# A transformer block with self and cross attention: preparing stage and first pass as one stage, and a new order of the loop

## The reference

```python
h1 = _ln(x, n1_g, n1_b)
x = _attn(h1, h1, q1, k1, v1, o1_w, o1_b, heads) + x
h2 = _ln(x, n2_g, n2_b)
x = _attn(h2, context, q2, k2, v2, o2_w, o2_b, heads) + x
h3 = _ln(x, n3_g, n3_b)
proj = h3 @ ff_w1 + ff_b1
a, g = jnp.split(proj, 2, axis=-1)
ff = a * jax.nn.gelu(g, approximate=False) @ ff_w2 + ff_b2
return ff + x
```

## Time and profile before

| | us |
|---|---|
| median of 3 runs | 1505.35 (1504.9 to 1515.25) |
| profiled execution | 1509.97 |
| its span, first to last instruction | 1508.2 |

### The profile page before, as it was taken

How to read it: one execution, slowest core, us unless ns; L and a number is a source line. 1 busy time by engine, 2 the same in 40 slices (tenths; PEclk the granted TensorE clock), 3 DMA queues, 4 the chain that set the end, 5 groups by cost and what they waited for, 6 DMA issues and landing times. The chain is left out here.

```text
span 1508.2 us, 36412 instructions
## 1 busy us (share of the span) xinstructions
PE 1390.9 (92%) x13777; PEld 1261.9 (84%) x13777; DVE 888.5 (59%) x2175; ACT 649.8 (43%) x1454; POOL 381.3 (25%) x473
## 2 busy tenths in 40 slices
PE   4599489999999999999999999999856999999999
PEld 1599467888888888889888888888746999999999
DVE  5666137777777677777777776776525434242421
ACT  2234123455555555555555555555433322223231
POOL 8221111212212212212122122122006423333341
PEclk9799779999999999999999999999867999999999
DMA  3365534444444455454453443442112010101000
GB/s 103 103 229 204 185 113 125 116 131 138 113 128 138 121 145 148 130 153 134 139 151 112 125 141 107 133 133 85 55 33 72 10 40 10 35 13 31 13 9 23
DMA packets 127678, 155.62 MB, mean 103 GB/s; under 512 B 29016, under 2 KB 123424, under 8 KB 127520
## 3 DMA queue, kind: packets, MB, share of 16 engines
q1 hardware_dynamic: 127520, 153.47, 34.1%
HBM read 62.98 MB, written 28.93 MB: 61 GB/s over the span
## 5 line engine op out<-in xcount | busy, mean ns | idle before, releaser
L684 DVE TENSOR_REDUCE neg_max<-score 100x1 f32<-100x361 f32 (+1 forms) x800 | 409.0, 535 | 212.3 <-PE score L509 107.7
L882 ACT ACTIVATE probs<-expin 120x400 f32<-120x400 f32 (+2 forms) x640 | 302.5, 504 | 144.1 <-PE expin L534 138.0
L534 PE MATMUL expin<-qs,ks 128*120 128x200 f32 (+2 forms) x1280 | 261.1, 293 | 12.1 <-DMA qs<-max_parts 10.8
L534 PEld LDWEIGHTS expin<-qs,ks 128*120 128x120 f32 (+2 forms) x1280 | 191.0, 184 | 54.0 <-ACT probs L882 26.1
L509 PE MATMUL score<-ks,qs 128*100 128x362 f32 x640 | 207.5, 349 | 6.4 <-DMA qs<-q_parts 3.6
L1626 DVE SCALAR_TENSOR_TENSOR hidden<-ps_a,b_cols,gelu 128x320 f32<-128x320 f32 x100 | 55.1, 551 | 169.0 <-PE ps_a L1549 165.2
L951 POOL TENSOR_TENSOR var_eps<-mv,eps 100x1 f32<-100x1 f32 x32 | 6.1, 192 | 526.8 <-DVE mv L751 526.8
L1792 POOL TENSOR_TENSOR hid_lo<-hidden,hid_hi 128x320 fp32r<-128x320 f32 x100 | 88.0, 881 | 130.9 <-ACT hid_hi L1703 130.9
L509 PEld LDWEIGHTS score<-ks,qs 128*100 128x100 f32 x640 | 103.2, 170 | 14.7 <-issue 10.4
L1715 ACT ACTIVATE gelu<-ps_g,b_cols 128x320 f32<-128x320 f32 x100 | 52.8, 528 | 137.6 <-PE ps_g L1549 137.5
L555 PE MATMUL attn<-probs,vc 120*17 120x100 f32 (+1 forms) x3840 | 111.2, 256 | 0.1
(11 more groups left out here) (180 smaller groups left out, 3070.0 us busy)
## 6 DMA issues: line engine op xcount, KB each, us to landing
ks<-kc_parts SPq DMA_DIRECT2D x192, 181.0 KB, 2.5
qk_dram<-qk_parts SPq DMA_DIRECT2D x32, 500.0 KB, 4.1
qs<-q_parts SPq DMA_DIRECT2D x192, 75.0 KB
ks<-qk_dram SPq DMA_DIRECT2D x96, 125.0 KB
qs<-qk_dram SPq DMA_DIRECT2D x192, 62.5 KB
ks<-kc_parts SPq DMA_DIRECT2D x96, 90.5 KB, 2.2
ctx_raw<-in_ctxT SPq DMA_DIRECT2D x32, 180.5 KB, 2.8
ctx_raw<-in_ctxT SPq DMA_DIRECT2D x64, 90.2 KB, 2.9
```

What stands on the lines that cost most here:

```text
L534: mm = pe.matmul(dst, ks[a][u][:, c, j0:j0 + n], qs[a][u][:, :, q_slot(c) if a == 2 else c, :], start=True, stop=True)
L684: nc.vector.tensor_reduce(dst, src, AX_X, ALU.max, negate=True).then_inc(max_made, 1)
L882: nc.scalar.activation(probs[e % NPT][0:n, :], expin[e % 2][0:n, 0:HG * N], ACT.Exp, scale=SCALE)\
```

## The change

**One stage in place of two.** `first_stage` loads x and the q, k and v weights at once. The first layer norm's gain and bias are now applied to the tokens (`scale`: two SCALAR_TENSOR_TENSORs with `g_rows` and `b_rows`), so the weights are only split. The other weights are loaded and split between the groups (`context_low`, `second_bias_low`, `q2_gain`, `out_low`, `q2_low`), and GpSimd clears the stacks between its small steps. The split features live in the room of the cross key stacks. After groups 3 and 5 the own stacks of batches 0 and 1 are loaded (`load_own`, 9 DMAs, also used in the loop), and the stage no longer waits for its last stores.

**The loop.** The cross queries are made as rows (8 matmuls of 320 columns), copied by ScalarE into `q2_rows` and turned by three transposes (`QT`). Cross scores are made for two heads at a time and self scores for ten, in one pair of banks; a maximum is taken over the pair, and the next pair waits for it. There are 11 `probs` instead of 8, context takes 2 DMAs instead of 3, and all orders are new.

**The feed-forward's start** no longer waits for the x2 stores before it, gets gain and bias rows ahead of the other tiles, waits for each vector by itself, loads ScalarE's Gelu table early, and adds `ff_b2` on GpSimd later.

```diff
-NW, NPT = 3, 8
+NW, NPT = 3, 11
...
+def load_own(sp, b, qk1_dram, v1_dram, qs, ks, vs, zeros, landed):
+    clear_max(sp, qs, zeros, landed)
+    src = qk1_dram[b]
...
+    sp.dma_start(vs[:].rearrange("p h d -> p (h d)"), v1_dram[b]).then_inc(landed, 16)
+OWN = 9
...
-        w_q2 = sb("w_q2", [P, 6, DP], F32R)
+        w_q2 = sb("w_q2", [P, 6, D], F32R)
...
-        score = [ctx.enter_context(nc.psum_tensor(f"score{i}", [P, 512], F32)) for i in range(2)]
+        score = ctx.enter_context(nc.psum_tensor("score", [P, 2, 512], F32))
...
-                sp.dma_start(ctx_raw[0:64, 1, 0:J], c[P:C]).then_inc(ctx_landed, 16)
-                sp.dma_start(ctx_raw[64:P, 1, 0:J], c[P:C]).then_inc(ctx_landed, 16)
+                sp.dma_start(ctx_raw[0:P, 1, 0:J], c[P:C].unsqueeze(0).broadcast_to([2, 64, J])).then_inc(ctx_landed, 16)
...
             def period(x, s, c, f, e):
+                load_qkv1(e)
+                place_max(1, f)
+                place_kc(c, 0)
                 load_x(f)
                 load_context(f)
-                load_qkv1(e)
-                place_kc(c, 0)
                 place_kc(c, 1)
-                place_kc(c, 2)
-                place_max(1, f)
                 place_q2(c)
                 place_max(2, s)
                 store_x2(x)
-            sp.wait_ge(zeros_set, 1)
-            load_qkv1(0)
+                place_kc(c, 2)
             for p in PERIODS:
-                period(*roles(p), p + 4 if p + 4 < B else None)
+                period(*roles(p), p + 4 if 1 < p + 4 < B else None)
                 if 8 <= p < 8 + FF // P:
                     load_w1(p - 8)
-            for u in range(2):
-                sp.wait_ge(x2_stored[u], 16 * (B // 2))
...
             def project_q2(b):
                 if b is None:
                     return
-                job = ("Q2", b, 0)
+                project(("Q2", b, 0), "T2", ("T2", b, 0), (hi_made["T2"], b + 1), [w_q2[:, i, :] for i in range(6)])
+            def turn_q2(b):
+                if b is None:
+                    return
+                job = ("QT", b, 0)
                 fill(job)
-                pe.wait_ge(*emptied(("T2", b, 0)))
+                pe.wait_ge(*emptied(("Q2", b, 0)))
                 for t in range(3):
-                    mm = project_turned(bank(job)[:, t * N:(t + 1) * N], "T2",
-                                        [w_q2[:, i, t * P:(t + 1) * P] for i in range(6)])
+                    mm = pe.transpose(bank(job)[:, t * N:(t + 1) * N], q2_rows[:, t * P:(t + 1) * P], identf[0:N, 0:N])
                 done(mm, job)
...
-            def score_bank(job):
-                i = SCORE_AT[job]
-                if i > 1:
-                    pe.wait_ge(max_made, i - 1)
-                return score[i % 2], score_full[i % 2]
-            def self_scores(b, g):
+            def empty_score(job):
+                if SCORE_AT[job]:
+                    pe.wait_ge(max_made, SCORE_AT[job])
+            def self_scores(b, i):
                 if b is None:
                     return
                 u = b % 2
-                if g == 0:
-                    pe.wait_ge(qkv1_landed[u], 16 * 11 * (b // 2 + 1))
-                dst, full = score_bank((1, b, g))
+                if i == 0:
+                    pe.wait_ge(qkv1_landed[u], 16 * OWN * (b // 2 + 1))
+                empty_score((1, b, i))
                 for a in range(2):
-                    for i in range(2):
-                        c, n0 = 2 * g + i, (2 * a + i) * N
-                        mm = pe.matmul(dst[0:N, n0:n0 + N], qs[1][u][:, a, c, :], ks[1][u][:, c, :],
+                    for k in range(HP // 2):
+                        c = HP // 2 * i + k
+                        mm = pe.matmul(score[0:N, a, k * N:(k + 1) * N], qs[1][u][:, a, c, :], ks[1][u][:, c, :],
                                        start=True, stop=True)
-                mm.then_inc(full, 1)
-            def cross_scores(b, hd):
+                mm.then_inc(score_full, 1)
...
+                empty_score((2, b, c))
+                for a in range(2):
+                    mm = pe.matmul(score[0:N, a, 0:JP], qs[2][u][:, a, q_slot(c), :], ks[2][u][:, c, :],
+                                   start=True, stop=True)
+                mm.then_inc(score_full, 1)
...
-                n = SCORE_AT[a, b, i]
-                src = score[n % 2]
-                dve.wait_ge(score_full[n % 2], n // 2 + 1)
+                dve.wait_ge(score_full, SCORE_AT[a, b, i] + 1)
                 if a == 1:
...
-                    k = q_slot(i // 2)
-                    dst, src = neg_max[2][b % 2][:, i % 2, k:k + 1], src[0:N, 0:J]
+                    dst, src = neg_max[2][b % 2][:, :, q_slot(i):q_slot(i) + 1], score[0:N, :, 0:J].unsqueeze(2)
                 nc.vector.tensor_reduce(dst, src, AX_X, ALU.max, negate=True).then_inc(max_made, 1)
...
+            def copy_q2(b):
+                if b is None:
+                    return
+                job = ("Q2", b, 0)
+                act.wait_ge(*filled(job))
+                if b:
+                    act.wait_ge(*filled(("QT", b - 1, 0)))
+                for dst, src in zip(spread_pairs(q2_rows[:], 4), natural_pairs(bank(job)[0:N])):
+                    ins = nc.scalar.copy(dst, src)
+                ins.then_inc(work_empty[WORK_AT[job][0]], 1)
...
+            load_x(0)
+            rows(g_rows, given["n1_g"], landed["rows"])
+            rows(b_rows, given["n1_b"], landed["rows"])
+            load_x(1)
+            load_x(2)
+            load_x(3)
+            for y, name in enumerate("qkv"):
+                weight(raw_qkv[:, y], given[name], landed[name])
+            for b in range(NB, 2 * NB):
+                load_x(b)
+            weight(raw_q2, given["q2"], landed["q2"])
+            for dst, v in ((gain, given["n2_g"]), (bias, given["n2_b"])):
+                weight(dst[:].unsqueeze(2), v.rearrange("(d a) -> d a", a=1), landed["columns"])
+            for a in (1, 2):
+                rows(o_b[a], given[f"o{a}_b"], landed["o_b"])
             for k in range(NK):
                 if k + 2 < NK:
-                    load(k + 2)
-                sp.wait_ge(qk_lo_made, 5 * (k + 1))
+                    for b in range((k + 2) * NB, (k + 3) * NB):
+                        load_x(b)
+                if k == 0:
+                    sp.wait_ge(w_lo_made, 3)
+                    for i, name in enumerate(("k2", "v2")):
+                        for j, src in enumerate(thirds_of(given[name])):
+                            sp.dma_start(raw_c[:, j, i * D:(i + 1) * D], src).then_inc(landed["c"], 16)
+                    weight(raw_o[1], given["o1"], landed["o1"])
+                if k == 5:
+                    sp.wait_ge(q2_lo_made, 1)
+                    weight(raw_o[2], given["o2"], landed["o2"])
+                sp.wait_ge(qk_lo_made, AT[k, 4] + 1)
                 for i in range(NB):
-                    sp.dma_start(qk1_dram[k * NB + i], parts[k % 2][:, i].rearrange("p l t n -> p l (t n)").bitcast(F32))\
-                        .then_inc(qk_stored[k % 2], 16)
+                    src = parts[k % 2][:, i].rearrange("p l t n -> p l (t n)").bitcast(F32)
+                    sp.dma_start(qk1_dram[k * NB + i].rearrange("l p m -> p l m"), src).then_inc(qk_stored[k % 2], 16)
                 for i in range(NB):
                     sp.wait_ge(v_made, k * NB + i + 1)
                     sp.dma_start(v1_dram[k * NB + i], v_rows[i][:].rearrange("p h d -> p (h d)"))\
                         .then_inc(v_stored[i], 16)
-            for u in range(2):
-                sp.wait_ge(qk_stored[u], 16 * NB * (NK // 2))
-            for i in range(NB):
-                sp.wait_ge(v_stored[i], 16 * NK)
+                if k in (3, 5):
+                    b = (k - 3) // 2
+                    if b == 0:
+                        sp.wait_ge(stacks_set, 1)
+                        sp.wait_ge(qk_stored[0], 16 * NB)
+                    sp.wait_ge(v_stored[b], 16)
+                    load_own(sp, b, qk1_dram, v1_dram, qs[1][b], ks[1][b], vs[b], zeros, qkv1_landed[b])
+            sp.wait_ge(landed["o_b"], 32)
...
+            pe.wait_ge(ident_step, 2)
             for b in range(NB):
                 turn_tile(b)
+            pe.wait_ge(w_lo_made, 2)
             for k in range(NK):
                 for t in range(5):
                     queries_keys(k, t)
                     if t < NB and k + 1 < NK:
                         turn_tile((k + 1) * NB + t)
+                if k == 0:
+                    pe.wait_ge(w_lo_made, 3)
+                if k == 2:
+                    second_bias()
...
             def scale(b):
                 i = b % NB
                 dve.wait_ge(stats_made, b + 1)
-                dve.wait_ge(rstd_made, b + 1)
                 if b > 1:
                     dve.wait_ge(turned, b - 1)
-                nc.vector.tensor_scalar(z[b % 2][:].rearrange("p (k d) -> p k d", k=2), twice(x[b % (2 * NB)][:]), mv[i][:, 0:1],
```

(46 more changed lines are left out.)

692 lines of the change are left out of this document (327 added, 365 removed).

## The result

| | median us | range | runs |
|---|---|---|---|
| kernel before | 1505.12 | 1503.33 to 1515.25 | 4 |
| changed kernel | 1458.95 | 1454.98 to 1466.39 | 4 |

The ratio is 0.969, 95% interval 0.963 to 0.974: faster by 3.1%, 46 us. The forecast was 1427, with a range of 1400 to 1460; two of the four runs, 1460.28 and 1466.39, lie outside it. The sign, and which places gain, came out as forecast; the gain is little over half of the 81 us that the sum gave. The profiled execution of the changed kernel was the longest of its four, so the spans understate its gain by a few us.

The account below looks back on a forecast made before the run. TensorE was taken to bound first pass and loop, waiting to count elsewhere. Terms of -16, -12, +2, -49 and -6 sum to -81 on the 1508.2 us span: 1427, own range 1408 to 1446, stated range 1400 to 1460.

Parts of the forecast that it names:

- term 1: Start and first pass: first product 39 us earlier, partly given back by +10, +7.6 and +5; sum -16, bounds -30 and -5.
- half clock in the first pass: First pass: TensorE falling to half clock, likeliest at the k2 and v2 stall, would make the prediction wrong; cost not summed.
- Rival 3: First pass: VectorE bounds it, locked by GpSimd up to 0.75 us a tile; start gain nothing, total 1443; chance 0.15.
- term 2: Gap between first pass and loop: shrinks from 16.43 to 4.4 us, -12, bounds -9 and -13.
- term 3: Loop's ramp: self scores in two halves and context loaded behind the maxima; +2 us, bounds -5 and +6.
- The step on the context: Ramp: context's DMA, 2.5 us of landing and 3.2 of splitting add +2 to +3.5 us before the first context keys.
- term 4: Loop: shorter Q2 and scores take the period from 27.76 to 26.1 us; -49, period bounds 25.2 (-76) and 27.3 (-14).
- rival 2: Loop: the single pair buffer takes the gain, period 27.5 us, loop only -9, total 1467; chance 0.13.
- rival 5: Loop: slower, as the next pair waits for its whole maximum; period 31.2 us at 0.6 a pair, total 1578; chance 0.03.
- term 5: Feed-forward's start: no wait for the last x2 store, earlier vectors, earlier table load; -6 us, bounds -3 and -7.

Follow-up runs that it names:

- the second experiment: Changed kernel with low parts of k2, v2 and o1 made after group 6 of the first pass, o2's after group 7; 1457.86 us, ratio 0.965.
- the best kernel: Changed kernel with context loads first, weights' low parts later, attn cleared first, GpSimd's w1 subtraction earlier, and unread products where TensorE waits; 1429.71 us, ratio 0.946.

## Why the prediction was right, and where it was not

**What bounds the kernel**: right. TensorE is busy 25.82 of 26.2 us in a steady period, as it was before.

**Start and first pass (term 1)**: -12.5 for -16. The first product came at 20.4, not 17; from there to the last values it took 22.9 us more than before, for 22.6 forecast. What was mis-sized in the start are landings. VectorE waited 3.58 us for the second tile, where I had put 1.0, and the weights of k landed at 17.6, not 9.5: the three issues took 5.19 us on the queue, not 0.57 each, and the last landed 7.5 us after them, not 1.9. The two chains end within 0.2 us of each other, and with the old scaling the second alone gives the same 20.37. The group of 14.9 was 14.76, and the experiment with the old scaling gives 13.55, so the cost of the second instruction (+1.4 forecast, +1.2 measured) was right in kind and size. The stall at k2 and v2 was 3.5 us for 3.3 forecast. I had said that half clock in the first pass would make the prediction wrong; it did fall, for 1.2 us of longer products. By that sign the prediction would be wrong; the cost was too small to decide it.

**Rival 3**, that GpSimd's short instructions hold VectorE's: out. The 32 instructions that make `z` took 617 to 620 ns, so no lock touched them. GpSimd's `rstd` took 0.55 us in most cases, but about 0.67 in ten and 0.94 and 1.03 in two: what time was lost, GpSimd lost.

**Gap (term 2)**: right, 11.3 for 12.

**Ramp (term 3)**: +6.9 for +2, outside its bounds of -5 and +6. The step on the context failed. I reckoned 2.5 us of landing, as the three DMAs of the kernel before have it, and 2 to 3.5 us in all; the new form lands after 6.7 us, the wait for `ctx_lo` was 6.41, and the clock stayed at half. The sum has nothing for two DMAs in place of three. The experiment with the context first takes 8.8 us off the ramp, with the new form left as it is.

**Loop (term 4)**: 24.2 for 49.4, which is 25 of the 37 us that are missing in all, by four steps.
- I took 27.76 for a period of the kernel before from a single one. 27.55 to 27.60 is what most last; with the mean of 27.62 that is 4 us too much.
- The scores. Q2 came out as forecast: its products take 1.38 us from start to next start instead of 2.69. Ten pairs take 3.8 us, not 3.6, and the single scores they replace 4.0, not 4.2; with the self scores this gave some 0.4 to 0.6 and not 1.0. TensorE's own work is 25.8, not 25.2. The waits were 0.4, not 0.9, and the period came out at 26.25 for 26.1 because two errors nearly cancel. 4 us.
- The context. I had gone through the DMAs that the new order makes later, the own stacks and the maxima, and found both in time. The context, which moves behind fourteen other issues and lands later after its own, I had looked at in the ramp alone. It is the last thing that the splitting waits for in 10 of 30 periods, TensorE waits up to 1.3 us behind it, and in two of them the clock falls; these two periods, 29.85 and 30.36, make 7.7 of the 12.7 us in all (773.95 less 29 times 26.25). With the context first they are gone.
- The two periods in which the loop runs out: +2.8 for -1.5. Their sum, 55.1 us in this trace, is 49.6 to 54.5 in the other traces of the new loop, so most of this miss is within what varies from run to run (52.3 and 50.8 in the two traces of the old loop).

**Rivals 2 and 5**: out. TensorE's waits for maxima in a steady period are too short to show, and single hand-over makes no difference. That the total came near rival 2's 1467 is no support for it.

**Feed-forward (term 5)**: -3.7 for -6. The wait for the vectors is gone, as forecast, but the second x tile lands at 1090.94 and is now what the second statistics wait for; and the time that the earlier vectors won is spent under GpSimd's subtraction. I had cited that exclusion, from the Trainium skill, SBUF — State Buffer, "Who interferes with whom", for the first pass, where it cost VectorE nothing, and not asked which instructions the earlier start would bring beside the subtraction of w1. The trace agrees with the rule there: 2.15 and 1.71 us, and 0.55 and 0.28 with the subtraction out of the way.

The forecast of faster by over 1% was right, and its mechanism with it: what bounds the loop, the shorter Q2, the earlier start and the smaller gap. That the range held the time is in part luck. No bound of it stands for a late context, every term came out worse than forecast, and the median is 1 us from the upper end. The sum had no term for the clock behind a new wait, and none for transfers of the steady loop that come late only sometimes.

## What to carry to other kernels

When a change reorders a queue, go through every transfer that now stands later in it, not only those that the change names, and ask in the steady state for the distance between landing and need; a margin of a microsecond is no margin where the issue moves by more than that from period to period (15 to 20 us into it here). When a change alters the form of a DMA, do not carry over the landing time of the old form: one that read its source twice took 7 us for bytes that had taken 3. Take a loop's period from many periods, not from one. And when an early start is won, look at what it now runs beside.

## What the hardware showed

**A wait of about 1 us can cost 4.** In three periods `ctx_lo` is late by 1.25 to 1.29 us (498.55, 578.57, 684.68), in a fourth by 1.14 (846.57). Behind 498.55, 578.57 and 846.57 the clock stays, and the period lasts 27.3 to 27.4; at 684.68 it falls to half for about 6 us, and the period lasts 30.36. The same happens in the first steady period with a wait of only 0.93 us (29.85), and twice in the steady loop of the second experiment's trace (30.4 and 30.72). With single scores waits of 1.59 and 1.38 us leave the clock at full. What tells the cases apart no row shows.

**The run-to-run spread goes mostly with the clock.** Of 13 runs of the kernel before on one chip the fastest (1503.30) has a mean clock of 0.972 and the slowest (1512.73) 0.957, if not strictly (1509.73 has 0.967, and over the ten runs with the feed-forward's start alone the two hardly go together); of the six of the best kernel 1424.03 has 0.986 and 1435.02 has 0.975. The last full interval of the new loop lasted 24.1 to 29.8 us in the ten traces without fillers at the loop's end; its clock was 0.60 where it took 29.15 and 0.86 where it took 24.64.

**Issuing is not a fixed price.** SyncE at the changed kernel's start (issue, its length, what is loaded):

```profile
3.11 1.74 SPq L1042 DMA_DIRECT2D raw<-in_q  x3
4.90 5.19 SPq L1042 DMA_DIRECT2D raw<-in_k  x3
10.13 4.71 SPq L1042 DMA_DIRECT2D raw<-in_v  x3
```

Three weight DMAs of the same shape hold SyncE 1.74 us for q, and 5.19 for k and 4.71 for v behind them. I had reckoned 0.57 us each from a mean over 28. What makes the later ones three times as long no run here separates; another order of the first loads was not tried.
